# Node phases with rings of eight chunks instead of four: eight input and output buffers, loops unrolled over eight chunks

## The reference

```python
edge_index = jnp.stack([src, dst])
x = _layernorm(x + _L0_gnn_ref(x, node_vec1, edge_attr_4, edge_attr_8, ..., src, dst), axis=-1)
x = _layernorm(x + _L1_gnn_ref(x, node_vec1, edge_attr_4, edge_attr_8, ..., src, dst), axis=-1)
x = _layernorm(x + _L2_gnn_ref(x, node_vec1, edge_attr_3, edge_attr_64, src, dst, ...), axis=-1)
x = _layernorm(x + _L3_gnn_ref(x, edge_attr_3, edge_attr_64, ..., src, dst), axis=-1)
```

## Time and profile before

| | us |
|---|---|
| median of 3 runs | 7069.88 |
| lowest and highest | 7062.25, 7082.83 |
| the profiled execution | 7065.26 |
| its span, first to last instruction | 7063.5 |
| busy: PE, DVE, POOL, ACT | 5499.5, 4436.8, 4522.4, 2754.1 |
| node phases 0, 1, 2, 3 by the trace | 554, 460, 1043, 611 |

### The profile page before, as it was taken

How to read it: one execution, slowest core, us unless ns; L and a number is a source line. 1 busy time by engine, 2 the same in 40 slices (tenths; PEclk the granted TensorE clock), 3 DMA queues, 4 the chain that set the end, 5 groups by cost and what they waited for, 6 DMA issues and landing times. The chain is left out here.

```text
span 7063.5 us, 125854 instructions
## 1 busy us (share of the span) xinstructions
PE 5499.5 (78%) x28355; PEld 4137.7 (59%) x28378; DVE 4436.8 (63%) x14951; ACT 2754.1 (39%) x5862; POOL 4522.4 (64%) x4862
## 2 busy tenths in 40 slices
PE   8889856679997867999655344469999969996665
PEld 6556556646667864556322144357777747775665
DVE  3566567744446975666577421248888857775666
ACT  6333356634444643444200000025555534443555
POOL 4688756658877877555277688856666668884222
PEclk9899988879999988999888666679999989998888
DMA  8566655546665643444311344432222225554554
GB/s 325 107 120 120 113 162 180 179 103 130 129 129 178 213 165 106 133 133 131 102 34 33 91 76 76 74 64 94 96 96 96 97 65 86 87 86 103 175 172 156
DMA packets 592064, 850.21 MB, mean 120 GB/s; under 512 B 220767, under 2 KB 340367, under 8 KB 587423
## 3 DMA queue, kind: packets, MB, share of 16 engines
q1 hardware_dynamic: 409502, 693.40, 30.4%
q0 software_dynamic: 182400, 154.98, 15.9%
HBM read 469.29 MB, written 377.54 MB: 120 GB/s over the span
## 5 line engine op out<-in xcount | busy, mean ns | idle before, releaser
L1143 POOL DMA_INDIRECT xg<-x,gidx x600 | 611.1, 1018 | 353.3 <-PE pt L1370 178.9
L318 POOL DMA_INDIRECT agg<-summed,cidx x400 | 644.0, 1610 | 191.7 <-issue 113.0
L2005 PE MATMUL pc_a<-msg_a,same_a 128*128 128x168 f32 x1000 | 263.5, 451 | 412.3 <-ACT summed_a L1992 354.5
L2005 PEld LDWEIGHTS pc_a<-msg_a,same_a 128*128 128x128 f32 x1000 | 250.4, 306 | 425.7 <-issue 294.5
L391 DVE TENSOR_TENSOR pr<-pf,ws 128x512 f32<-128x512 f32 x200 | 138.3, 691 | 526.9 <-PE pf L478 386.3
L1327 ACT ACTIVATE ob<-po 128x416 f32<-128x416 f32 (+1 forms) x400 | 201.5, 504 | 547.5 <-PE po L1399 378.1
L2187 POOL TENSOR_TENSOR rs_n<-ve_n,wsb 128x4 f32<-128x4 f32 x98 | 98.7, 1007 | 473.5 <-DVE nm_n L2175 473.5
L1154 POOL DMA_INDIRECT agg<-summed,cidx x200 | 324.1, 1620 | 79.0 <-issue 58.5
L1261 DVE TENSOR_TENSOR pr<-pf,ws 128x512 f32<-128x512 f32 (+1 forms) x250 | 172.2, 689 | 319.5 <-ACT ws L1313 218.8
L1951 POOL DMA_INDIRECT agg<-summed_a,cidx_a x200 | 318.3, 1592 | 70.8 <-issue 59.7
L1871 PE MATMUL pm_m<-arow_m,ones_m 128*128 128x512 bf16 x400 | 163.7, 501 | 215.7 <-DVE apart_m L1811 148.6
(11 more groups left out here) (338 smaller groups left out, 18369.7 us busy)
## 6 DMA issues: line engine op xcount, KB each, us to landing
ar_n<-agg SPq DMA_DIRECT2D x194, 322.0 KB
agg<-zero SPq DMA_DIRECT2D x50, 768.0 KB
ar_n<-agg SPq DMA_DIRECT2D x97, 384.0 KB
agg<-zero SPq DMA_DIRECT2D x50, 672.0 KB
ar_n<-agg SPq DMA_DIRECT2D x97, 336.0 KB
agg<-zero_h SPq DMA_DIRECT2D x25, 1288.0 KB, 5.4
agg<-zero SPq DMA_DIRECT2D x50, 644.0 KB
x<-xn_n SPq DMA_DIRECT2D x97, 324.0 KB, 2.2
```

The source lines that it names most:

```text
L318: pool.indirect_dma_start(agg, bass.IndirectOffsetOnAxis(ap=cidx[r][:, t:t + 1], axis=0), summed[u][:, t, :], None, compute_op=ALU.add).th ...
L1143: pool.indirect_dma_start(xg[s][r][:, t, 0:XR], None, x, bass.IndirectOffsetOnAxis(ap=gidx[s][r][:, t:t + 1], axis=0)).then_inc(gathered[r ...
L2005: last = pe.matmul(pc[:, t, 0:W], same[u][:, s, t * P:(t + 1) * P], msg[u][:, s, :], start=(s == t), stop=(s == T - 1))
```

## The change

A second ring size `RN` = 8 is set beside `R` = 4 and used in the four node phases. `pipeline` takes the ring as an argument; `node_pipeline` gives it 8 and a head of 16 positions, so that the loop body is eight positions long. `xr`, `ar` and `xn` get eight buffers each, `loaded` and `stored` eight semaphores. `load(c)` waits for `y` and its fellows of chunk `c - 8` in place of `c - 4`. The lags of all stages, the order of the stages, and all tiles with two buffers stay as they are; `y` of phase 1 and `xx` of phase 2 keep four buffers, and pairs of chunks in phase 1 keep two.

```diff
+RN = 8
...
-def pipeline(eng, n, head, stages):
...
-    tail = (n - 1) // R * R
+def pipeline(eng, n, head, stages, ring=R):
...
+    tail = (n - 1) // ring * ring
...
             if 0 <= c < n:
-                f(c, c % R, c // R, LASTP if c == NC else P)
+                f(c, c % ring, c // ring, LASTP if c == NC else P)
...
-    with eng.Fori(head // R, tail // R) as j:
-        for q in range(R):
+    with eng.Fori(head // ring, tail // ring) as j:
+        for q in range(ring):
             for lag, f in stages:
-                f(R * j + (q - lag), (q - lag) % R, j + (q - lag) // R, P)
+                f(ring * j + (q - lag), (q - lag) % ring, j + (q - lag) // ring, P)
...
 def node_pipeline(eng, stages):
-    pipeline(eng, NC + 1, 2 * R, stages)
+    pipeline(eng, NC + 1, 2 * RN, stages, RN)
```

In each node phase (phase 3 stands for all):

```diff
-        xr = each(R, sb, "xr", [P, T, D])
-        ar = each(R, sb, "ar", [P, T, 192])
+        xr = each(RN, sb, "xr", [P, T, D])
+        ar = each(RN, sb, "ar", [P, T, 192])
...
-        xn = each(R, sb, "xn", [P, T, D])
+        xn = each(RN, sb, "xn", [P, T, D])
...
-        loaded = each(R, sem, "loaded")
+        loaded = each(RN, sem, "loaded")
...
-        stored = each(R, sem, "stored")
+        stored = each(RN, sem, "stored")
...
             def load(c, r, k, parts):
-                sp.wait_ge(y_ok, due(c - 3))
+                sp.wait_ge(y_ok, due(c - RN + 1))
...
-            for r in range(R):
-                sp.wait_ge(stored[r], 16 * ((NC - r) // R + 1))
+            for r in range(RN):
+                sp.wait_ge(stored[r], 16 * ((NC - r) // RN + 1))
```

What keeps four or two buffers is indexed anew, as here in phases 1 and 2:

```diff
-                    f(2 * k + r // 2, r // 2, k, r)
+                    f(RN // 2 * k + r // 2, r // 2 % 2, k, r)
...
-                v = r // 2
+                v = r // 2 % 2
...
-                    a.activation(xn[r][:, t, 0:D], y[r][:, t, :], ACT.Identity, ...)
+                    a.activation(xn[r][:, t, 0:D], y[r % R][:, t, :], ACT.Identity, ...)
...
-                pool.tensor_tensor(xx[r][:], x1[u][:], xr[r][:, :, 0:D], ALU.add).then_inc(xx_ok, 1)
+                pool.tensor_tensor(xx[r % R][:], x1[u][:], xr[r][:, :, 0:D], ALU.add).then_inc(xx_ok, 1)
```

More of the change, by code:

```diff
@@ L521, in node_phase_01 @@
         each = lambda count, f, n, *a: [f(f"{n}{q}", *a) for q in range(count)]
-        xr = each(R, sb, "xr", [P, T, XW])
-        ar = each(R, sb, "ar", [P, T, 161])
+        xr = each(RN, sb, "xr", [P, T, XW])
+        ar = each(RN, sb, "ar", [P, T, 161])
         xta = each(2, sb, "xta", [P, B])
@@ L540, in node_phase_01 @@
         nr = each(2, sb, "nr", [P, T])
-        xn = each(R, sb, "xn", [P, T, XW])
+        xn = each(RN, sb, "xn", [P, T, XW])
         pta = each(2, ps, "pta", [P, B])
@@ L790, in node_phase_1 @@
         nr = each(2, sb, "nr", [P, 2 * T])
-        xn = each(R, sb, "xn", [P, T, XL])
+        xn = each(RN, sb, "xn", [P, T, XL])
         pta = each(2, ps, "pta", [P, B])
@@ L909, in sums @@
                 for t in range(T):
-                    v.scalar_tensor_tensor(y[r][:, t, :], pk[u][:, t, 0:D], a3[:, bass.ds(c * T + t, 1)], xr[r][:, t, 0:D], ALU.mult, ALU.add).then_inc(y_ok, 1)
+                    v.scalar_tensor_tensor(y[r % R][:, t, :], pk[u][:, t, 0:D], a3[:, bass.ds(c * T + t, 1)], xr[r][:, t, 0:D], ALU.mult, ALU.add).then_inc(y_ok, 1)
             def moments(c, r, k, parts):
                 n = (r % 2) * T
-                s = st[r // 2]
-                v.wait_ge(m_ok, due(NM * (2 * k + r // 2 - 1)))
+                s = st[r // 2 % 2]
+                v.wait_ge(m_ok, due(NM * (RN // 2 * k + r // 2 - 1)))
                 for t in range(T):
                     v.wait_ge(y_ok, T * c + t + 1)
-                    v.bn_stats(s[:, n + t, 0, :], y[r][:, t, 0:S0]).then_inc(st_ok, 1)
-                    v.bn_stats(s[:, n + t, 1, :], y[r][:, t, S0:D]).then_inc(st_ok, 1)
+                    v.bn_stats(s[:, n + t, 0, :], y[r % R][:, t, 0:S0]).then_inc(st_ok, 1)
+                    v.bn_stats(s[:, n + t, 1, :], y[r % R][:, t, S0:D]).then_inc(st_ok, 1)
             def join(p, h, k, r):
@@ L2204, in node_phase_2 @@
         each = lambda count, f, n, *a: [f(f"{n}{q}", *a) for q in range(count)]
-        xr = each(R, sb, "xr", [P, T, XL])
-        ar = each(R, sb, "ar", [P, T, AW[2]])
+        xr = each(RN, sb, "xr", [P, T, XL])
+        ar = each(RN, sb, "ar", [P, T, AW[2]])
         den = each(2, sb, "den", [P, T, H])
@@ L2277, in load @@
             def load(c, r, k, parts):
-                sp.wait_ge(x1_ok, due(T * (c - 3)))
+                sp.wait_ge(x1_ok, due(T * (c - RN + 1)))
                 fence(sp)
-                sp.wait_ge(xx_ok, due(c - 3))
+                sp.wait_ge(xx_ok, due(c - RN + 1))
                 fence(sp)
-                sp.wait_ge(col_ok, due(c - 3))
+                sp.wait_ge(col_ok, due(c - RN + 1))
                 fence(sp)
@@ L2485, in output @@
                     v.wait_ge(o_ps, 2 * c + t // 2 + 1)
-                    v.scalar_tensor_tensor(y[u][:, t, :], pk[:, t, 0:D], at(c, t), xx[r][:, t, :], ALU.mult, ALU.add).then_inc(y_ok, 1)
+                    v.scalar_tensor_tensor(y[u][:, t, :], pk[:, t, 0:D], at(c, t), xx[r % R][:, t, :], ALU.mult, ALU.add).then_inc(y_ok, 1)
                 v.wait_ge(s2_ok, 8 * c)
```

14 lines of the change are left out of this document (7 added, 7 removed).

## The result

The changed kernel takes 7117.15 us (median of 3 runs, 7112.02 to 7118.84) against 7069.88: ratio 1.0059, 95% interval 1.0045 to 1.0073. It is slower by 47 us, outside the range. The profiled execution has a span of 7117.0 us, 53.5 more than before.

The account below looks back on a forecast made before the run. It took TensorE and VectorE to bound phase 2, chains of waits phases 0 and 3, GpSimd phase 1. Gains of 13 + 3 + 10 + 2 = 28 us less 20 for fetches gave -8: 7062 us, range 7034 to 7094.

Parts of the forecast that it names:

- Half the loop ends, phase 2, -10 us: Phase 2: 12 fewer loop ends at 0.82 us each save 10 us, with 6 us as the lower end.
- The fetch, +20 us: VectorE, phase 2: the longer body is no longer resident; nine jumps back wait 2.2 us each for instructions, 20 us more.
- Rival 2: VectorE's jumps in phase 2: a dear fetch; one at 4.8 us gives +15, two in a row +58; chance 0.20.
- Rival 1, all resident: All loop bodies stay in instruction memory, so no fetch cost: 28 us less, 7042; chance 0.32.
- Load's own wait, phase 3, -13 us: Phase 3: dropping the load's wait for `y` four chunks back saves 12 us, 13 with one earlier load at the start.
- loop ends there, -2: Phase 3: 12 fewer loop ends at some 0.4 us on SyncE, a third of it counting, save 2 us.
- The circle through `xn`: Phase 3: load, transposes, `skip`, `y`, variance, `xn`, store, later load; spans three chunks, stays, taken as tight.
- Both ends that I set, 0 and 17: Phase 3: bounds in us on the gain from the load's earlier wait; 12 was taken.
- SyncE's order: SyncE runs in program order, so each load still leaves about 0.7 us behind an older chunk's store, despite eight buffers.
- rival 3: Loads truly run ahead; phase 3 falls from 6.1 towards 5.5 us a chunk, 59 us less, about 7010; chance 0.06.
- Phases 0 and 1, 0 and -3: Phase 0 gains nothing; phase 1 saves 3 us by 12 fewer loop ends at 0.24 us; earlier loads give 0 in both.
- The stores' side and the code's bytes, 0: Waiting for stores eight chunks back saves 0 us; the added code's transfers, under 0.6 MB, cost nothing.

Follow-up runs that it names:

- after_vec_written_out: Changed kernel with VectorE's phase 2 written out in full, without a loop; ratio 1.0032 to the kernel before the change.
- p2_rest8: Kernel before the change with phase 2 loops of eight positions on all engines but VectorE, four buffers and old waits; ratio 1.0024.
- p2_vec8: Kernel before the change with a phase 2 loop of eight positions on VectorE only, four buffers and old waits; ratio 1.0003.
- p2_ring6: Kernel before the change with six buffers and loops of six positions in phase 2 alone; ratio 1.0038.
- p3_run_ahead: Kernel before the change with the whole change in phase 3 alone, and SyncE's store there moved from lag 4 to lag 7; ratio 0.9818.

## Why the prediction was wrong

It forecast 8 us less and 47 more were measured, 53.5 in the profiled executions. By its own steps:

- *Half the loop ends, phase 2, -10 us.* This step failed, in sign. It took the gap of 10.71 us at the loop's end in the earlier trace rows as the price of the end. That gap is the collision of `hat` and `xx`, lost by VectorE. Before, it does fall on each of the 22 loop ends, but it is not their price: it can fall on any chunk, and after the change five gaps of eight are near 10.7, without a loop's end in them. What an end brought was the three chunks at the short gap behind it. With half the ends the chunks at 10.70 became the rule: 12.3 us more (after_vec_written_out), 12.6 with the other engines' loops alone (p2_rest8). The bracket in that step ("a VectorE operation that falls on another of GpSimd's") named it and drew no conclusion. A swing of 22 us. What the ends themselves give back shows in p2_vec8: nine gaps longer by 0.92 us are 8.3 us, the phase is longer by 3.5, so 12 of VectorE's ends are worth some 4.8 by this estimate, half of what I had.
- *The fetch, +20 us.* Right in place and in kind: VectorE alone, 179 packets where 180 were forecast. That the size, 23.6 us, is near it is luck: there are two stops at a jump, not one, 2.6 us together and not 2.2 for one, and 13.4 of the 23.6 hang on the second, which ten instructions ahead of the loop take away. In p2_vec8 the fetch costs 8.3 us. Rival 2's "two fetches one after another" is what happened, at a quarter of its price, as the slow `hat` covers 1.3 us (so it is not true that nothing hides it on VectorE) and the later packets come while the body runs. The Trainium skill, page "Runtime: NRT & Kernel Launch", section "Instruction fetch mechanics", gives TensorE 2048 instructions, and the trace agrees in that its 1121 stay. For VectorE the Trainium skill gives 512 instructions in blocks of 256; 381 are fewer than 512, and the trace of p2_ring6 shows them fetched all the same, in packets of 8 KB. Whether they lay within two such blocks no trace shows. Rival 1, all resident, falls with the fetch.
- *Load's own wait, phase 3, -13 us; loop ends there, -2.* The first failed, in sign: -15 in all against +12.3 in the profiled executions, the largest error of the sum. The circle through `xn` was the tight one, as argued, but the wait for `y` wasn't a cost within it. It kept the chunks apart; without it `xn` is waited for 98.4 us longer, more than the 69.4 that went. Both ends that I set, 0 and 17, were on the side of a gain: a wait that goes may also leave the pipeline worse, and that was not among the bounds. The sign I had for the rest of the change in phase 3 was right: 602.9 with eight buffers and the old wait.
- *SyncE's order.* Right. The load leaves 0.6 us behind the store after the change (6703.44, 6704.06), and rival 3 doesn't come about. But its price, 59 us, was far too small: p3_run_ahead gains 146.5 us of phase 3. I had held phase 3 against phase 0's 5.5 us a chunk, which has its own circle; without waits for loads a chunk takes 471.6 / 98 = 4.8 us.
- *Phases 0 and 1, 0 and -3.* They took 0.1 and 0.2 us more. Phase 0's circle on GpSimd is free of loads, as argued. That of phase 1 is not: with the loads truly ahead the phase falls by 17 to 22 us. The change left this alone, since its store lag of six kept the order.
- *The stores' side and the code's bytes, 0.* Nothing speaks against it. 5.0 us more between the node phases weren't forecast and weren't looked into.

Right terms would have been 23.6 + 12.3 + 12.3 = 48.2 us; with 0.3 in phases 0 and 1 and 5.0 between the phases they make the 53.5. The 12.3 of phase 3 is the least sure of them, as only 1 to 3 us of it show on the slower chips.

## What to carry to other kernels

More buffers bring little (here 0.15%) while one in-order queue issues each load behind an old store: move the store's lag first, then count buffers. Before a loop body is made longer, count its instructions on each engine and look for packets of the instruction queues inside the loop. And a wait in a steady pipeline may be what keeps its chunks apart: bound its removal on the side of a loss too.

## What the chip showed that was not expected

- VectorE's loop bodies of 261 and 283 instructions stay resident; those of 381 and 501 are fetched at every jump, in 8 KB packets. The first instruction comes 2.8 us behind the branch, where it is 0.3 us without a fetch, and in the changed kernel another stop of 1.4 us follows behind a second packet. Ten added instructions ahead of the loop took the second stop away, 13.4 us in nine jumps.
- Two operations of VectorE and GpSimd that start within 0.04 us of each other decide by their order over 0.47 us, and the order changes with the length of other engines' loops; taking the two apart gave 26.3 us in 98 chunks.
